# A state-space and expert kernel: the next group's product cut into pieces between dependent VectorE steps, two small steps moved to ScalarE

## The reference

```
block 1: xn = rmsnorm(x); xb, z = split(xn @ in_proj)            # 512 channels each
         xc = silu(conv over 4 tokens(xb));  dt, B, C = split(xc @ x_proj)
         dt = softplus(dt * w + b)
         h[t] = exp(dt*A) * h[t-1] + dt * B[t] * xc[t]            # 512 channels x 16 states
         y = (sum over states of h*C + xc*D) * silu(z) @ out_proj + residual
block 2: scores = sigmoid(x @ gate_weight)                        # 16 experts in 4 groups
         the 2 best groups, in them the 4 best experts; weights = scores / their sum
         y = sum over the 4 of weight * (silu(x@G_e) * (x@U_e)) @ D_e
```

## Time and profile before

| | us |
|---|---|
| median of 3 runs | 2573.94 (2572.68 to 2574.6) |
| profiled execution, its own time | 2572.43 |
| its span, first to last instruction | 2570.6 |
| VectorE busy | 2375.5 (92%) |
| TensorE matmuls busy | 2361.5 (92%) |
| ScalarE busy | 1602.5 (62%) |
| GpSimd busy | 1494.2 (58%) |

### The profile page before, as it was taken

One profiled execution on the slowest core, in us unless ns is written; L12 is line 12 of the kernel. 1 busy time (PEld: TensorE's weight loads), 2 busy tenths in 40 slices (PEclk: granted clock), 3 DMA queues, 4 the chain that ended last, 5 costly groups with the idle time before them and its releaser, 6 DMA issues.

```text
span 2570.6 us, 26578 instructions
## 1 busy us (share of the span) xinstructions
PE 2361.5 (92%) x8416; PEld 1172.0 (46%) x8416; DVE 2375.5 (92%) x2831; ACT 1602.5 (62%) x3186; POOL 1494.2 (58%) x531
## 2 busy tenths in 40 slices
PE   6556899999999999999999999999999999988998
PEld 2112354544545454454545445454544545443555
DVE  4989999999999999999999999999999999999642
ACT  6566567666766667676676667666666766654341
POOL 0555556657566665756666575656657566666522
PEclk9778899999999999999999999999999999998999
DMA  4442433535353453534344353534535353443232
GB/s 151 168 147 77 152 117 131 169 98 187 114 161 120 137 172 100 185 114 156 124 142 167 98 186 116 163 117 139 170 100 184 116 158 114 143 157 93 76 77 63
DMA packets 172919, 344.48 MB, mean 134 GB/s; under 512 B 16075, under 2 KB 81388, under 8 KB 164460
## 3 DMA queue, kind: packets, MB, share of 16 engines
q1 hardware_dynamic: 164860, 334.93, 39.0%
q0 software_dynamic: 7920, 7.87, 2.3%
HBM read 291.35 MB, written 51.38 MB: 133 GB/s over the span
## 4 chain that ended last, share of the span: by engine, by line
DVE 63%; issue 18%; PE 10%; ACT 8%; DMA 0%; POOL 0%; DVEq 0%; ACTq 0%; POOLq 0%
DVE hs L1085 30%; DVE hs L1065 14%; DVE th L1185 5%; DVE th L1180 5%; PE MY L511 2%; PE Gp L493 2%; PE Up L501 2%; DVE XC L1027 2%; ACT dA L604 1%; ACT SZ L677 1%; DVE SZ L1092 1%; ACT L604 1%; DVE DX L1049 1%; ACT L677 1%; PE FP L418 1%
## 5 line engine op out<-in xcount | busy, mean ns | idle before, releaser
L947 POOL TENSOR_TENSOR hs<-hs,Cb 128x2048 f32<-128x2048 f32 x256 | 1159.2, 4528 | 160.3 <-DVE hs L1065 159.7
L604 ACT ACTIVATE dA<-dtr,A 128x512 f32<-128x512 f32 x1024 | 700.8, 689 | 732.8 <-DVE hs L1085 730.3
L932 POOL TENSOR_TENSOR th<-th,cmb 128x512 f32<-128x512 f32 x256 | 325.8, 1275 | 899.5 <-DVE hs L1065 805.0
L1085 DVE TENSOR_TENSOR_SCAN hs<-dA,carry,hs 128x512 f32<-128x512 f32 x512 | 626.7, 1264 | 5.9 <-ACT dA L604 5.5
L1085 DVE TENSOR_TENSOR_SCAN hs<-dA,hs 128x512 f32<-128x512 f32 x512 | 595.0, 1202 | 14.2 <-ACT dA L604 13.7
L1065 DVE TENSOR_TENSOR hs<-dxr,Bb 128x2048 f32<-128x2048 f32 x255 | 586.1, 2298 | 1.6 <-PE Y L527 1.6
L493 PE MATMUL Gp<-x2T,Wgu 128*128 128x512 f32 x1024 | 510.5, 621 | 24.8 <-DVE th L1180 24.1
L511 PE MATMUL MY<-Wdn,th 128*128 128x256 f32 x2048 | 485.9, 381 | 0.8 <-POOL th L932 0.8
L501 PE MATMUL Up<-x2T,Wgu 128*128 128x512 f32 x1024 | 482.5, 593 | 0.0
L511 PEld LDWEIGHTS MY<-Wdn,th 128*128 128x128 f32 x2048 | 383.4, 190 | 136.2 <-issue 92.8
L493 PEld LDWEIGHTS Gp<-x2T,Wgu 128*128 128x128 f32 x1024 | 177.1, 191 | 353.4 <-issue 277.6
(11 more groups left out here) (180 smaller groups left out, 1754.0 us busy)
## 6 DMA issues: line engine op xcount, KB each, us to landing
dxr<-dx_d SPq DMA_DIRECT2D x128, 512.0 KB, 7.1
cmb<-cm_d SPq DMA_DIRECT2D x256, 256.0 KB, 3.6
dtr<-dt_d SPq DMA_DIRECT2D x63, 1024.0 KB, 5.5
Wdn<-in_w_dn SPq DMA_DIRECT2D x256, 128.0 KB, 3.4
Bb<-bc_d SPq DMA_DIRECT2D x64, 256.0 KB, 3.0
Cb<-bc_d SPq DMA_DIRECT2D x64, 256.0 KB, 3.4
dt_d<-XB SPq DMA_DIRECT2D x15, 1024.0 KB, 4.3
dx_d<-DX SPq DMA_DIRECT2D x15, 1024.0 KB, 5.8
```

Of the source, the lines that this page charges most:

```text
L604: act.activation(dA[h % 2][:, :], dtr[:, M % 2, beta, :], ACT.Exp, scale=A[:, k:k + 1]).then_inc(s_dA, 1)
L932: pool.tensor_tensor(th[:, q % NTH, :], th[:, q % NTH, :], cmb[:, q % 2, :], ALU.mult).then_inc(m_a, 1)
L947: pool.tensor_tensor(hs[:, G % NH, :, :], hs[:, G % NH, :, :], Cb[:, s, :].unsqueeze(1).broadcast_to([P, NBETA, CH]), ALU.mult).then_inc(s ...
L1085: dve.tensor_tensor_scan(hv, dA[h % 2][:, :], hv, first, ALU.mult, ALU.add).then_inc(s_h, 1)
```

## The change

Four things are changed.

1. `inputs(G, k, parts)` can write the k-th of 2, 4 or 8 parts of a group's product. `conv` issues two halves between its three steps; `newton` issues four quarters after its steps 1, 3, 5 and 7 (in `norms` and in `p_scale2`, not in the last stages' own); the routing issues eight eighths of 256 columns. The single `inputs(G+1)` at the end of slots 2, 3, 4, 6 and 9 goes. The semaphore `s_u` rises with the last part.
2. `y_out` of slot 9 is issued right behind the routing's first instruction (a reciprocal), where it stood behind the last.
3. The variance in `p_scale2` moves to ScalarE, behind `p_squares2` in slot 5; the scaling into `comb` moves to ScalarE, as four instructions of 16 columns behind `f_softplus` in slot 9 (the factor 0.5 goes into the copy `p_cmT`). The waits for `comb` follow it.
4. On ScalarE in slot 12 the expert's tanh stands ahead of the two `decay` of slot 13, not behind them.

```diff
@@ ScalarE
             def p_squares2(p):
                 ...
+                act.wait_ge(p_act.sem, p_act.at(p - 1, 'sq2'))
+                act.activation(p_w[:, 0, :], b_s[:, :], ACT.Copy, scale=1.0 / DM, bias=LN_EPS).then_inc(p_act.sem, 1)
+            def p_comb(p):
+                c = p - 1
+                act.wait_ge(p_dve.sem, p_dve.at(c, 'wr'))
+                if c > 0:
+                    act.wait_ge(fp_full, filled(p - 1, 'ct'))
+                for b in range(TB):
+                    ins = act.activation(comb[:, b * NE:(b + 1) * NE], picked[:, b, 0:NE], ACT.Copy, scale=R[:, 7, 2 * TB + b:2 * TB + b + 1])
+                ins.then_inc(p_act.sem, 1)
+                if g == 12 and experts_at(G):
+                    tanh(experts_at(G)[0])
                 if 0 <= G + 1 < NGRP:
                     decay((G + 1) * NBETA)
                     decay((G + 1) * NBETA + 1)
-                if experts_at(G):
+                if g != 12 and experts_at(G):
                     tanh(experts_at(G)[0])
                     ...
+                if R_ and g == 9:
+                    p_comb(p)
@@ VectorE
-            def newton(steps, c, tag, v, y, a):
+            def newton(steps, c, tag, v, y, a, part=lambda k: None):
                 dve.tensor_scalar(y.bitcast(I32), v.bitcast(I32), ...).then_inc(steps.sem, 1)
+                part(0)
                 done('guess')
                 ...
                     dve.scalar_tensor_tensor(out=xc, in0=XB[:, m, k:k + CH], ...).then_inc(f_dve.sem, 1)
+                    if k < HIST - 1:
+                        inputs(p * GPC + 3 + m, k, 2)
-            def inputs(G):
+            def inputs(G, k=0, parts=1):
                 ...
+                if parts <= NBETA:
+                    n = NBETA // parts
+                    u, dx_, B_ = (hs[:, G % NH, k * n:(k + 1) * n, :], dxr[:, M % 2, k * n:(k + 1) * n, :], Bb[:, s, :]...)
+                else:
+                    beta, half = divmod(k, 2)
+                    t = slice(half * CH // 2, (half + 1) * CH // 2)
+                    u, dx_, B_ = (hs[:, G % NH, beta, t], dxr[:, M % 2, beta, t], Bb[:, s, t])
+                ins = dve.tensor_tensor(u, dx_, B_, ALU.mult)
+                if k == parts - 1:
+                    ins.then_inc(s_u, 1)
             def p_scale2(p):
-                dve.wait_ge(p_act.sem, p_act.at(c, 'sq2'))
-                variance(p_w[:, 0, :], b_s[:, :]).then_inc(p_dve.sem, 1)
-                dve.wait_ge(p_dve.sem, p_dve.at(c, 'Bw1'))
-                newton(p_dve, c, 'q', p_w[:, 0, :], p_w[:, 1, :], p_w[:, 2, :])
+                dve.wait_ge(p_act.sem, p_act.at(c, 'var2'))
+                newton(p_dve, c, 'q', p_w[:, 0, :], p_w[:, 1, :], p_w[:, 2, :], lambda k: inputs(p * GPC + 7, k, 4))
                 ...
                 dve.reciprocal(score, den).then_inc(p_dve.sem, 1)
+                if 0 <= p < NC:
+                    y_out(p * GPC + 7)
                 ...
                 dve.reciprocal(wr, ws).then_inc(p_dve.sem, 1)
-                if c > 0:
-                    dve.wait_ge(fp_full, filled(p - 1, 'ct'))
-                done('wr')
-                dve.scalar_tensor_tensor(out=per_b(comb[:, :]), in0=chosen, scalar=0.5, in1=wide(wr), ...).then_inc(p_dve.sem, 1)
@@ VectorE, the slots
-                if 0 <= G + 1 < NGRP:
+                if not (G + 1 >= 0 and (F and g in (2, 3) or g == 4 or R_ and g in (6, 9))):
                     inputs(G + 1)
```

More of the change, by code:

```diff
@@ L480, in p_comb @@
                 bank_free(p, 'ct')
-                pe.wait_ge(p_dve.sem, p_dve.at(c, 'comb'))
+                pe.wait_ge(p_act.sem, p_act.at(c, 'comb'))
                 for b in range(TB):
@@ L985, in newton @@
                 dve.tensor_tensor(a, a, v, ALU.mult).then_inc(steps.sem, 1)
+                part(1)
                 done('t0')
@@ L989, in newton @@
                 dve.scalar_tensor_tensor(out=y, in0=a, scalar=1.875, in1=y, op0=ALU.add, op1=ALU.mult).then_inc(steps.sem, 1)
+                part(2)
                 done('y0')
@@ L993, in newton @@
                 dve.tensor_tensor(a, a, v, ALU.mult).then_inc(steps.sem, 1)
+                part(3)
                 done('t1')
@@ L1044, in f_dx @@
                 if in_p(p):
-                    dve.wait_ge(p_dve.sem, p_dve.at(p - 1, 'comb'))
+                    dve.wait_ge(p_act.sem, p_act.at(p - 1, 'comb'))
                 if c == 0:
@@ L1049, in f_dx @@
                     dve.tensor_tensor(DX[:, :, :], dt, XC[:, c % 2, :, :], ALU.mult).then_inc(f_dve.sem, 1)
-            def inputs(G):
+            def inputs(G, k=0, parts=1):
+                if not 0 <= G < NGRP:
+                    return
                 c, M, s = (G // GPC, G // NSIG, G % NSIG)
@@ L1057, in inputs @@
                     return
-                if s == 0:
-                    for k in range(2):
-                        dve.wait_ge(ld_dx[2 * (M % 2) + k], 16 * (M // 2 + 1))
-                if M % MT == 0:
-                    dve.wait_ge(ld_B[s], 16 * (c + 1))
-                if G >= NH:
-                    dve.wait_ge(s_y, G - NH + 1)
-                dve.tensor_tensor(hs[:, G % NH, :, :], dxr[:, M % 2, :, :], Bb[:, s, :].unsqueeze(1).broadcast_to([P, NBETA, CH]), ALU.mult).then_inc(s_u, 1)
+                if k == 0:
+                    if s == 0:
+                        for half in range(2):
+                            dve.wait_ge(ld_dx[2 * (M % 2) + half], 16 * (M // 2 + 1))
+                    if M % MT == 0:
+                        dve.wait_ge(ld_B[s], 16 * (c + 1))
+                    if G >= NH:
+                        dve.wait_ge(s_y, G - NH + 1)
+                if parts <= NBETA:
+                    n = NBETA // parts
+                    u, dx_, B_ = (hs[:, G % NH, k * n:(k + 1) * n, :], dxr[:, M % 2, k * n:(k + 1) * n, :], Bb[:, s, :].unsqueeze(1).broadcast_to([P, n, CH]))
+                else:
[5 more added lines that the diff above has]
+                    ins.then_inc(s_u, 1)
             def scan(G, beta):
@@ L1150, in done @@
                     dve.wait_ge(p_dve.sem, p_dve.at(c, name))
+                inputs(p * GPC + 10, 2, 8)
                 done('tmp')
@@ L1154, in route_experts @@
                 ins.then_inc(p_dve.sem, 1)
+                inputs(p * GPC + 10, 3, 8)
                 done('top')
@@ L1168, in route_experts @@
                 dve.scalar_tensor_tensor(out=chosen, in0=per_b(eq), scalar=1.0, in1=per_b(score), op0=ALU.add, op1=ALU.mult).then_inc(p_dve.sem, 1)
+                inputs(p * GPC + 10, 6, 8)
                 done('w')
                 dve.tensor_reduce(ws, picked[:, :, :], AX.X, ALU.add).then_inc(p_dve.sem, 1)
+                inputs(p * GPC + 10, 7, 8)
                 done('ws')
                 dve.reciprocal(wr, ws).then_inc(p_dve.sem, 1)
-                if c > 0:
-                    dve.wait_ge(fp_full, filled(p - 1, 'ct'))
-                done('wr')
-                dve.scalar_tensor_tensor(out=per_b(comb[:, :]), in0=chosen, scalar=0.5, in1=wide(wr), op0=ALU.mult, op1=ALU.mult).then_inc(p_dve.sem, 1)
             def expert_gate(q):
@@ L1256, in _ @@
                     route_experts(p)
-                if g == 9 and 0 <= G - 2 < NGRP:
+                if g == 9 and not R_ and 0 <= G - 2 < NGRP:
                     y_out(G - 2)
```

14 lines of the change are left out of this document (9 added, 5 removed).

## The result

The change makes the kernel slower: 2580.64 us (median of 10 runs, 2579.39 to 2582.1) against 2572.67 (10 runs, 2567.65 to 2574.6), ratio 1.0034, 95% interval [1.0026, 1.0043]. The forecast was 2550, and the range ended at 2563. The profiled span is 2578.7 us, against 2570.6.

The account below looks back on a forecast made before the run. VectorE was taken to bound the chunks, TensorE the end. Routing 14.4, `p_scale2` 5.2, `conv` and `norms` 3.9 plus 0.3 and 0.3, less 0.3, gave 23.8 us: 2573.9 to 2550, range 2541 to 2563.

Parts of the forecast that it names:

- The step that failed: GpSimd (POOL) gets `s_u` at the same distance from the next gate or up to 0.7 us earlier; no cost counted.
- doesn't do what it says: Rival, chance 0.04: pieces fill waits but are themselves held up, or ScalarE's slots 9 and 12 give it back; 2570 to 2574.
- VectorE bounds the chunks: VectorE sets the chunks' pace with TensorE close behind: 294.4 and 290.7 us busy of 300; TensorE sets the end.
- A filled wait saves 0.12, a cut costs 0.067: On VectorE, work put into a wait on an own result saves 0.12 us; each extra instruction costs 0.067.
- The rival that pieces hide nothing: Rival, chance 0.05: VectorE empties at each instruction, so a cut costs 0.147 us and fills nothing; 25 us lost, 2599.
- `p_scale2` 0.46, `norms` 0.28 a chunk: VectorE's net gain in us: slot 6 from the variance leaving and four filled waits, slot 4 without the variance.
- The wait foretold for the decay of slot 9: First-half chunks: VectorE needs the decay for slot 9's third scan; slack 0.24 against slot 6's 0.46, about 0.22 arrives.
- `conv` in second-half chunks only: Slots 2 and 3: 0.28 us a chunk, arriving in second-half chunks; in first-half ones it becomes a wait for TensorE.
- Early `y_out`: TensorE's wait at slot 10 goes and becomes one for `th`: TensorE's waits of 2.15 and 1.08 us for `y_out` at slot 10's head vanish; one for `th` replaces them.
- ScalarE's moves cost nothing there, 8 us on VectorE: Variance (0.18 us) and `comb` scaling (0.35) leave VectorE in each chunk; ScalarE's slack of 0.4 absorbs the copies.
- The tanh at 0: Slot 12's tanh ahead of two decays: between -0.1 and +0.15 us per chunk, taken as 0.
- The sum without the hold: All terms together: 23.8 us gained, giving 2550; the forecast's own range 2544 to 2556, over all cases 2541 to 2563.

Follow-up runs that it names:

- e1: The changed kernel, with GpSimd also waiting in slots 5 and 7 for the last small step (`n_nb`, `p_nb`): 2547.11 us.
- e5: The kernel before, nothing cut, with the whole product issued ahead of `newton`'s last step in `norms` and `p_scale2`: 2610.48 us.
- e9: e1 with the tanh of slot 12 put back behind the two decays of slot 13: 2545.73 us.
- e11: e9 with `conv` uncut, its three steps together and the whole product behind them: 2549.86 us.
- e4: The kernel before, nothing cut, with the whole product directly ahead of the last small step (`n_nb`, `p_nb`) in slots 4 and 6: 2573.45 us.
- e6: The changed kernel, with `p_nb` in slot 6 computed by four one-column instructions, each reading one tensor and a pointer scalar: 2567.69 us.

## Why the prediction was wrong

The step that failed is one sentence of it: "No DMA is issued at another place, and POOL gets `s_u` at the same distance from the next gate or up to 0.7 earlier." I took the earlier semaphore as harmless, and priced the last step of both chains at its old distance. What the runs show in its place: in slots 4 and 6 the earlier `s_u` starts GpSimd's multiply 0.03 to 0.04 us before that last step can start, and the step is held for the multiply's 1.27 us, or its 4.5 us where no expert's multiply comes first. That makes 43.7 us more in VectorE's records, of which 33.5 reach the end (after 2580.64 against e1 2547.11). Of the rest, 5.6 are waits that e1 has and the changed kernel has not (for TensorE's `Y` 11.5 against 7.6, for `dA` 21.5 against 19.8); where the last 4.6 go I didn't follow. The case "doesn't do what it says" named GpSimd's reads, but at 2570 to 2574 and as a hold of the pieces; they aren't held.

Point by point:

- *VectorE bounds the chunks.* Right. The holds of 31 small steps came out as time for the most part (e5: 37.3 of 43.5 us; after: 33.5 of 43.7).
- *A filled wait saves 0.12, a cut costs 0.067.* Right: routing to the gate 5.22 against 5.3, the eighths 7.8 us against 7.4. The rival that pieces hide nothing is dead. The rule it came from doesn't hold for these small steps: independent ones start inside the record of the one before (0.14 apart at 0.22 long, 1170.95 and 1171.09). The Trainium skill (VectorE: DVE Perf Modes, "The DRAIN you can't avoid") says this itself in the same section, "A next op that is not held starts earlier", which the prediction left out.
- *`p_scale2` 0.46, `norms` 0.28 a chunk.* Wrong as they stood. Slot 6's chain took 4.63 us (1141.93 to 1146.56) where it was forecast at 3.6. With the hold removed the sign and nearly the size come back (3.7 us for both roots' quarters, 4.6 to 6.2 forecast). The wait foretold for the decay of slot 9 in a first-half chunk is there: 0.16 in e1 (scan at 1293.12), with 0.22 forecast. A slip stands in that term: a slack of 0.24 against 0.46 lets 0.24 arrive and leaves 0.22 as the wait, and not the reverse; it is worth 0.1 us in the sum.
- *`conv` in second-half chunks only.* Right in the steady part. From the variance at slot 4 of one first-half chunk to that of the chunk four later VectorE takes 592.36 us in e9 (1248.86 to 1841.22) and 593.05 in e11 (1251.42 to 1844.47), with `conv` cut in four chunks against none: 0.34 a pair, where one chunk of each pair at 0.28 was forecast. And with `conv` uncut the wait for TensorE in slot 5 of a first-half chunk shrinks from 0.68 to 0.27, so there the cuts only lengthen the wait. Of the 4.1 us, 1.8 are there by the first such variance (508.25 against 510.06) and 3.1 by the last (1989.52 against 1992.63). So the early chunks gained what the prediction left out, and the last 1 us I didn't follow.
- *Early `y_out`: TensorE's wait at slot 10 goes and becomes one for `th`.* Right in kind. Its worth was 3.5 and not 1.8 us: I priced the filled wait and took TensorE's earlier start at nothing, with VectorE as the bound. That the difference is TensorE's start is argued, not shown; it is little more than what these figures are good to.
- *ScalarE's moves cost nothing there, 8 us on VectorE.* 7.1 measured. The tanh at 0: right (e9).
- *The sum without the hold.* 23.8 us forecast, 26.3 (e1) and 27.5 (e9) measured; both are inside the range given.

## What to carry to other kernels

When a change lets a semaphore rise earlier, look past the one who waits for it: list what still stands behind the raising instruction on the same engine, and what the woken engine will do to it. In these runs a VectorE step with two SBUF tensors that came up 0.03 to 0.04 us behind the start of a GpSimd multiply took that multiply's whole length, with 4 columns as with 16; put such steps ahead of the semaphore that wakes GpSimd. Filling the waits of a dependent chain with pieces of independent work does pay here: by the prices that the sum used, which the parts bear out roughly, 0.12 us for each wait against 0.067 for each cut.

## What the runs showed of the hardware that I had not expected

- Whether a step is held is decided by 0.2 us. The same step is 0.17 long when it starts 0.16 before GpSimd (e4) and 1.26 when it starts 0.04 behind (e5).
- It works the other way round as well. In slot 2 `conv`'s third step (two SBUF tensors) starts 0.15 before GpSimd's multiply, which is then 1.72 long and not 1.27 (with `conv` uncut, in e11, it is 1.27 again, at 1096.60). Timelines of VectorE and of GpSimd, after:

```profile
...
1103.39 0.73 DVE L1046 SCALAR_TENSOR_TENSOR XC<-XB,Cols,XC 128x512 f32<-128x512 f32 x1
...
```

```profile
...
1103.54 1.72 POOL L947 TENSOR_TENSOR th<-th,cmb 128x512 f32<-128x512 f32 x1 [3.73 <-DVE hs L1096]
...
```

- Not every GpSimd instruction holds. While GpSimd issues its DMA to `out` (1.30 us from 1168.68, after), the routing's step `DX<-DX,Ebias` with two SBUF tensors takes 0.21 at 1169.73.
- A step with one tensor input can be held too, and the kernel before shows it already. The variance in slot 6, 4 columns with two constants, took 0.14 in the earlier trace rows, when GpSimd's multiply was ending. In seven first-half chunks it comes 0.25 before that end, takes 0.28, and ends 0.03 behind GpSimd (1283.19 and 1283.16). With the variance on ScalarE, `newton`'s first step, with two constants as well, stands there and takes 0.29 (1291.36, after), so the move didn't save the hold. VectorE and GpSimd, before:

```profile
...
1282.91 0.28 DVE L999 TENSOR_SCALAR p_w<-b_s 128x4 f32<-128x4 f32 x1
...
```

```profile
...
1278.63 4.53 POOL L947 TENSOR_TENSOR hs<-hs,Cb 128x2048 f32<-128x2048 f32 x1
...
```

- In the last stage the variance `z_w<-z_s`, of the same form, takes 0.84 and ends (2495.86) with GpSimd's multiply (2494.57 to 2495.83); before it took 0.17, when GpSimd was done. In e6 the steps of one column with a factor from a tensor were not held. Which of the two differences matters, the width or the kind of scalar, no run tells. VectorE and GpSimd, after:

```profile
...
2495.02 0.84 DVE L1018 TENSOR_SCALAR z_w<-z_s 128x4 f32<-128x4 f32 x1 [2.13 <-ACT XB L614]
...
```

```profile
...
2494.57 1.26 POOL L947 TENSOR_TENSOR th<-th,cmb 128x512 f32<-128x512 f32 x1 [17.11 <-DMA cmb<-cm_d]
...
```

- A held instruction's record shows the hold as its own length; no view lists it as a wait. It is found only by setting the mean of a line beside the same line of before.
